# Decoder layer with eight routed experts: routed rows read in squares of 32 and transposed on VectorE

## Reference

```python
x = x + _L0_attn_ref(_layernorm(x), w_qkv, w_out)          # windowed, rotary, 16 heads of 8
x = x + _L0_xattn_ref(_layernorm(x), ctx_1024, Wq, bq, Wk, bk, Wv, bv, Wo, bo, 1)
x = x + _L0_ffn_ref(_layernorm(x), gate_w, w1, w2)

def _L0_ffn_ref(x, gate_w, w1, w2):                        # E = 8 experts, F = 512, TOP_K = 2
    probs = jax.nn.softmax(x @ gate_w, axis=-1)
    topw, topi = jax.lax.top_k(probs, TOP_K)
    topw = topw / topw.sum(axis=-1, keepdims=True)
    combine = (jax.nn.one_hot(topi, E) * topw[..., None]).sum(axis=-2)
    for each expert i:
        h = jax.nn.gelu(x @ w1[i], approximate=False)
        acc = acc + combine[..., i, None] * (h @ w2[i])
    return acc
```

## Time and profile before

| | |
|---|---|
| median of 3 runs | 544.39 us (540.61 to 544.9) |
| profiled execution | 540.55 us, its span 538.7 us |
| mean granted TensorE clock | 0.982 of full speed |
| TensorE busy | 479.2 us, 89% of the span |
| VectorE busy | 380.0 us, 71% |
| ScalarE busy | 338.8 us, 63% |
| GpSimd busy | 306.3 us, 57% |
| DMA queue of SyncE | 35712 packets, 24.69 MB, 16.1% of 16 engines' span |

### The profile page before, as it was taken

One profiled execution on the slowest core, in us unless ns is written; L12 is line 12 of the kernel. 1 busy time (PEld: TensorE's weight loads), 2 busy tenths in 40 slices (PEclk: granted clock), 3 DMA queues, 4 the chain that ended last, 5 costly groups with the idle time before them and its releaser, 6 DMA issues.

```text
span 538.7 us, 30462 instructions
## 1 busy us (share of the span) xinstructions
PE 479.2 (89%) x11885; PEld 397.7 (74%) x11885; DVE 380.0 (71%) x1342; ACT 338.8 (63%) x980; POOL 306.3 (57%) x415
## 2 busy tenths in 40 slices
PE   2589899999999899989899999889987999999992
PEld 2367677777776677767677777666876999999991
DVE  5456688888886734667777777887777666666884
ACT  3357587787786767777888888788532444444440
POOL 2434344544554534357778777776677555555652
PEclk9999999999999988999999999999998999999997
DMA  8312111111111000001111011122122322227264
GB/s 235 89 43 62 41 58 43 56 58 44 54 58 43 29 13 12 15 28 45 33 32 43 30 40 37 34 53 55 49 76 86 93 68 73 74 69 264 56 178 138
DMA packets 40970, 35.09 MB, mean 65 GB/s; under 512 B 6445, under 2 KB 37295, under 8 KB 40896
## 3 DMA queue, kind: packets, MB, share of 16 engines
q1 hardware_dynamic: 35712, 24.69, 16.1%
q0 software_dynamic: 4320, 8.53, 4.7%
q10 hardware_dynamic: 864, 0.86, 0.6%
HBM read 18.63 MB, written 11.68 MB: 56 GB/s over the span
## 4 chain that ended last, share of the span: by engine, by line
PE 79%; issue 7%; DVE 5%; DMA 4%; ACT 2%; POOL 1%; SPq 1%; DVEq 0%; POOLq 0%; ACTq 0%
PE p_scores L1217 11%; PE p_probsT L630 11%; PE p_att_bank L620 8%; PE p_scores L513 7%; PE p_qk L1226 5%; PE p_probsT L1226 5%; PE p_scores L558 5%; PE p_v_bank L583 4%; PE p_scores L506 4%; PE p_att_bank L568 3%; PE p_qk L525 3%; PE p_qk L534 2%; PE p_v_bank L599 2%; PE p_att_bank L935 2%; PE p_qk L526 1%
## 5 line engine op out<-in xcount | busy, mean ns | idle before, releaser
L759 POOL TENSOR_TENSOR k_heads<-qk,consts 128x512 f32<-128x512 f32 x64 | 66.8, 1043 | 95.9 <-DVE qk L821 60.2
L1278 POOL DMA_INDIRECT expert_results<-weighted,result_at x71 | 74.2, 1044 | 53.2 <-DVE weighted L1264 42.7
L657 ACT COPY probsT<-p_probsT 128x512 f32<-128x512 f32 x128 | 75.5, 590 | 23.7 <-PE p_probsT L630 23.4
L860 DVE TENSOR_REDUCE shift<-p_scores 128x8 bf16<-128x512 f32 (+1 forms) x128 | 73.8, 618 | 22.0 <-PE p_scores L513 21.4
L1217 PE MATMUL p_scores<-gotT,w_now 128*128 128x128 f32 x568 | 76.8, 279 | 7.0 <-ACT gotT L1243 4.8
L630 PE MATMUL p_probsT<-consts,probs 128*128 128x128 f32 x512 | 80.7, 281 | 0.4
L663 ACT ACTIVATE probs<-p_scores 128x512 f32<-128x512 f32 x128 | 77.8, 608 | 0.5 <-PE p_scores L558 0.4
L1240 ACT ACTIVATE hidden<-p_scores 128x512 f32<-128x512 f32 x71 | 42.4, 597 | 54.8 <-PE p_scores L1217 54.8
L1217 PEld LDWEIGHTS p_scores<-gotT,w_now 128*128 128x128 f32 x568 | 69.7, 193 | 9.1 <-ACT gotT L1243 6.2
L1003 POOL DMA_INDIRECT sent_rows<-row,slot_u x64 | 64.7, 1011 | 16.6 <-issue 15.2
L716 ACT COPY values<-p_v_bank 32x128 f32<-32x128 f32 x256 | 68.4, 267 | 2.3
(11 more groups left out here) (160 smaller groups left out, 962.8 us busy)
## 6 DMA issues: line engine op xcount, KB each, us to landing
got<-sent_rows SPq DMA_DIRECT2D x71, 66.0 KB, 1.8
swapped<-raw SPq DMA_DIRECT2D x64, 64.0 KB, 1.9
w<-w_in SPq DMA_DIRECT2D x32, 128.0 KB, 2.3
back<-expert_results SPq DMA_DIRECT2D x7, 512.0 KB, 6.0
ctxT<-ctxT_in SPq DMA_DIRECT2D x32, 64.0 KB, 1.9
x<-x_in SPq DMA_DIRECT2D x4, 448.0 KB, 9.4
out<-x SPq DMA_DIRECT2D x7, 256.0 KB, 3.6
expert_results<-weighted,result_at POOLq DMA_INDIRECT x71, 2.4
```

What stands on the lines that cost most here:

```text
L657: nc.scalar.copy(probsT[:, 4 * half:4 * half + 4, :], p_probsT[:, :].rearrange("p (m q) -> p m q", q=P)).then_inc(s_pT, 1)
L759: nc.gpsimd.tensor_tensor(k_heads[:, :, BLK:], qk[:, 1:2, :].to_broadcast([P, G, P]), cv(C_HEAD, G).unsqueeze(2).to_broadcast([P, G, P]), ...
L860: nc.vector.tensor_reduce(shift[:, half * 8:half * 8 + 8], p_scores[:, half * 8:half * 8 + 8, low:WIN], AX.X, ALU.max).then_inc(s_max, 1)
L1278: nc.gpsimd.indirect_dma_start(out=results, out_offset=bass.IndirectOffsetOnAxis(ap=result_at[:, slot:slot + 1], axis=0), in_=weighted[:, ...
```

## The change

The transpose of a block's rows is split between the DMA and VectorE. The tile `got` is now [128, slot, 4, 32]: SyncE reads the 32 columns i of all 128 rows into the partitions 32i to 32i+31, where the partition counts the row within a group of 32, and the free index the group and the column. VectorE's transpose, which works on squares of 32x32, then turns each square in its place and gives `gotT` [feature, row]. The last four columns go to a tile of their own, `got_cols`. So a block has five DMAs, and the semaphore of a slot counts 80 instead of 16. TensorE's transpose, the PSUM tile for it and ScalarE's copy fall away. The multiply by the gate's weight moves from VectorE to ScalarE, and the cast of the result row numbers moves up to block c+2, with a semaphore of its own, `s_at`.

```diff
-        got = sb("got", [P, U, ROW])
+        got = sb("got", [P, U, NBLK, BLK])
+        got_cols = sb("got_cols", [P, U, ROW - P])
...
+        GOT = 16 * (NBLK + 1)
...
             if c >= U:
                 eng.wait_ge(s_y, n + 1 - U)
+                eng.wait_ge(s_at, n + 1 - U)
             first = eng.value_load(table_at(1, n), min_val=0, max_val=E * CAP)
-            eng.dma_start(got[:, slot, :], sent[bass.ds(first, P), :]).then_inc(s_got[slot], 16)
+            for i in range(NBLK):
+                eng.dma_start(got[i * BLK:(i + 1) * BLK, slot, :, :],
+                              sent[bass.ds(first, P), i * BLK:(i + 1) * BLK].rearrange("(j a) b -> a j b", a=BLK)).then_inc(s_got[slot], 16)
+            eng.dma_start(got_cols[:, slot, :], sent[bass.ds(first, P), P:ROW]).then_inc(s_got[slot], 16)
...
         def expert_pe(h, c, _):
...
-            if block_there(h, c, 2):
-                nc.tensor.wait_ge(s_got[(c + 2) % U], 16 * h + 16 * ((c + 2) // U + 1))
-                wait(nc.tensor, s_gT, n + 1)
-                nc.tensor.transpose(p_gotT[c % 2], got[:, (c + 2) % U, 0:P], ident).then_inc(s_gTraw, 1)
...
         def expert_act(h, c, _):
...
-            if block_there(h, c, 2):
-                nc.scalar.wait_ge(s_gTraw, n + 3)
-                nc.scalar.copy(gotT[:, c % 2, :], p_gotT[c % 2]).then_inc(s_gT, 1)
+            if block_there(h, c, -1):
+                slot = (c - 1) % U
+                nc.scalar.wait_ge(s_down, n)
...
+                nc.scalar.wait_ge(s_got[slot], GOT * h + GOT * ((c - 1) // U + 1))
+                nc.scalar.activation(weighted[:, slot, :], p_y[(c - 1) % 2], ACT.Copy, scale=got_cols[:, slot, 0:1]).then_inc(s_y, 1)
...
         def expert_dve(h, c, cols):
...
                 nc.vector.tensor_copy(w1_now[:, c % 2, :], w1[:, bass.ds(at, F)]).then_inc(s_w1_now, 1)
-            if block_there(h, c, -1):
-                slot = (c - 1) % U
-                nc.vector.wait_ge(s_down, n)
...
-                nc.vector.wait_ge(s_got[slot], 16 * h + 16 * ((c - 1) // U + 1))
-                nc.vector.tensor_copy(result_at[:, slot:slot + 1], got[:, slot, P + 1:P + 2])
-                nc.vector.tensor_scalar(weighted[:, slot, :], p_y[(c - 1) % 2], got[:, slot, P:P + 1], None, ALU.mult).then_inc(s_y, 1)
+                slot = (c + 2) % U
+                nc.vector.wait_ge(s_got[slot], GOT * h + GOT * ((c + 2) // U + 1))
+                nc.vector.transpose(gotT[:, c % 2, :], got[:, slot, :, :].rearrange("p j b -> p (j b)")).then_inc(s_gT, 1)
...
+                    nc.vector.wait_ge(s_back[slot], 16 * h + 16 * ((c + 2) // U))
+                nc.vector.tensor_copy(result_at[:, slot:slot + 1], got_cols[:, slot, 1:2]).then_inc(s_at, 1)
...
         def expert_pool(h, c, _):
...
+                nc.gpsimd.wait_ge(s_at, n)
                 nc.gpsimd.wait_ge(s_y, n)
```

More of the change, by code:

```diff
@@ L236, in build @@
         p_hidden = [p_scores[:, i * G:(i + 1) * G, :].rearrange("p g k -> p (g k)") for i in range(2)]
-        p_gotT = [p_scores[:, i * G, :] for i in range(2, 4)]
         p_y = [p_qk[:, 0:P], p_probsT[:, 0:P]]
@@ L273, in build @@
         s_back = [sem(f"results_sent{i}") for i in range(U)]
-        s_gTraw, s_gT, s_up, s_gelu = sem("gotT_in_psum"), sem("gotT_made"), sem("hidden_in_psum"), sem("hidden_made")
+        s_gT, s_at, s_up, s_gelu = sem("gotT_made"), sem("result_at_made"), sem("hidden_in_psum"), sem("hidden_made")
         s_w1_now, s_w2_now, s_down, s_y = sem("w1_copied"), sem("w2_copied"), sem("y_in_psum"), sem("y_weighted")
@@ L1240, in expert_act @@
                 nc.scalar.activation(hidden[:, half, :], p_hidden[half][:, :], ACT.Gelu).then_inc(s_gelu, 1)
-            if block_there(h, c, 2):
-                nc.scalar.wait_ge(s_gTraw, n + 3)
-                nc.scalar.copy(gotT[:, c % 2, :], p_gotT[c % 2]).then_inc(s_gT, 1)
+            if block_there(h, c, -1):
+                slot = (c - 1) % U
+                nc.scalar.wait_ge(s_down, n)
+                if not isinstance(h, int) or c - 1 >= U:
+                    nc.scalar.wait_ge(s_back[slot], 16 * h + 16 * ((c - 1) // U))
+                nc.scalar.wait_ge(s_got[slot], GOT * h + GOT * ((c - 1) // U + 1))
+                nc.scalar.activation(weighted[:, slot, :], p_y[(c - 1) % 2], ACT.Copy, scale=got_cols[:, slot, 0:1]).then_inc(s_y, 1)
         def expert_dve(h, c, cols):
@@ L1255, in expert_dve @@
                 nc.vector.tensor_copy(w1_now[:, c % 2, :], w1[:, bass.ds(at, F)]).then_inc(s_w1_now, 1)
-            if block_there(h, c, -1):
-                slot = (c - 1) % U
-                nc.vector.wait_ge(s_down, n)
-                if not isinstance(h, int) or c - 1 >= U:
-                    nc.vector.wait_ge(s_back[slot], 16 * h + 16 * ((c - 1) // U))
-                nc.vector.wait_ge(s_got[slot], 16 * h + 16 * ((c - 1) // U + 1))
-                nc.vector.tensor_copy(result_at[:, slot:slot + 1], got[:, slot, P + 1:P + 2])
-                nc.vector.tensor_scalar(weighted[:, slot, :], p_y[(c - 1) % 2], got[:, slot, P:P + 1], None, ALU.mult).then_inc(s_y, 1)
+                slot = (c + 2) % U
+                nc.vector.wait_ge(s_got[slot], GOT * h + GOT * ((c + 2) // U + 1))
+                nc.vector.transpose(gotT[:, c % 2, :], got[:, slot, :, :].rearrange("p j b -> p (j b)")).then_inc(s_gT, 1)
+                if not isinstance(h, int) or c + 2 >= U:
+                    nc.vector.wait_ge(s_back[slot], 16 * h + 16 * ((c + 2) // U))
+                nc.vector.tensor_copy(result_at[:, slot:slot + 1], got_cols[:, slot, 1:2]).then_inc(s_at, 1)
             if block_there(h, c, 1):
@@ L1295, in _ @@
             pe.wait_ge(s_probs, 4 * B)
-            for c in (-2, -1, 0):
-                expert_pe(0, c, None)
+            expert_pe(0, 0, None)
             go(steps[B - 1], ALL)
@@ L1331, in _ @@
             steps = {c: kinds[1][1](0, c) for c in range(B - 1, B + 4)}
-            expert_act(0, -2, None)
-            expert_act(0, -1, None)
             nc.scalar.activation(unread[0:1, :], eps[0:1, 0:1], ACT.Gelu)
```

## The result

| | before | after |
|---|---|---|
| median | 544.64 us (540.61 to 546.51, 4 runs) | 630.67 us (630.35 to 631.83, 4 runs) |
| profiled execution, its span | 540.55 us, 538.7 us | 630.95 us, 629.1 us |

The ratio is 1.1655, 95% interval 1.1598 to 1.1713: 86 us slower. The forecast was 620 us, range 602 to 660.

What follows compares the result with a forecast made beforehand. TensorE bounded the expert stage at 1.895 us a block; after, SyncE at 3.21. Last block's DMA 586.6, with pads, read-back and loop 600.2, landing and hand-over 602.5, tail 616.1, clock 617.6; forecast 620 us, range 602 to 660.

Steps and rivals of the forecast that it cites:

- from there SyncE alone sets the pace: Row reads after the first issue at 359.80 us: SyncE's issuing bounds every block, 3.21 us each; chance 0.82.
- 1.097 + 4 x 0.528: SyncE's time per block: 1.097 us for today's single read plus 0.528 for each of four added DMAs, 3.21 us.
- the wait for a second semaphore: SyncE's table load also waits for VectorE's index cast; costed at nothing, since eight slots lie between.
- The loop: The 24 blocks in SyncE's loop have register operations of their own, about 0.1 us each, 2.4 us together.
- The end: Tail from the last block's first projection to the span's end: 13.6 us, expected to stay as before.
- swing between its two levels: TensorE in the expert stage, idle 1.4 us of each 3.2, alternates between low and full clock and keeps up.
- the 19 us for the low level throughout: TensorE at low clock for the 53 blocks after the pads: 0.36 us each, 19 us, used for the range.
- the clock's term: 1.5 us added to the sum for TensorE running the last block at the low clock level.
- the hand-over of the last block: After the last read lands, transpose and hand-over to TensorE take 0.5 us.
- The packets: Rival: 720 small packets a block make the DMA engines the bound, from 71 ns a packet; chance 0.09.
- The hidden issue: Rival: SyncE's added issues stay hidden, each under 0.17 us, and only TensorE's gain shows: 534.5 us; chance 0.04.
- the faster rival: SyncE's issues stay hidden behind TensorE's work, leaving its gain of 6.0 us, so 534.5 us; chance 0.04.

## Why the prediction was right, and where its sum was off

**The bound.** The step "from there SyncE alone sets the pace" held from the first read to the last, and it was tested from both sides: five issues alone cost 1.16 to 1.18, the rest alone gives 0.987.

**The pace of SyncE.** The sum had 3.21 us a block from 1.097 + 4 x 0.528, and measured are 3.16 undisturbed: the stripes issue in 317 ns, not 333, while the wait for a second semaphore was indeed free. The loop adds 0.16, not 0.1. The last issue nevertheless came at 611.0, not 600.2. The term that was missing: between 358.94 and 609.02 us lie 70 blocks; without the pads (8.8) and the read-back (2.8) that is 238.5 us, or 3.41 each, while 46 at 3.16 and 24 at 3.32 are 225. The other 13.4 us are stretches: 8.0 of them are issues that lasted longer than their medians, as from 366.31 on (up to 1.79 us for one), the rest is time between issues. The row of before had shown a maximum of 873 ns; the median was taken for all.

**The end.** Timeline of the last block after the change:

```profile
612.62 0.31 DVE L1265 STREAM_TRANSPOSE gotT<-got 128x128 f32<-128x128 f32 x1 [1.92 <-DMA got_cols<-sent_rows]
...
612.98 0.97 PEld L1223 LDWEIGHTS p_scores<-gotT,w_now 128*128 128x128 f32 x8 [1.34 <-DVE gotT L1265]
...
617.55 0.97 POOL L1284 DMA_INDIRECT expert_results<-weighted,result_at  x1 [0.30 <-issue]
...
622.13 0.80 SPq L446 DMA_DIRECT2D back<-expert_results  x2
```

From the last first projection to the end it is 16.1 us, where 13.6 were carried over from the earlier trace rows. The chain differs in one place: from the start of the last result's scatter to the read-back that waits for it are 4.6 us (617.55 to 622.13), before 2.3 (529.66 to 531.93). Two read-backs of 512 KB are issued 3.5 us ahead of it now; before, they had gone 10 us ahead. That they delayed it is a reading, not tested.

**The clock.** The forecast that TensorE would swing between its two levels and keep up held. These are first projections behind the pads, behind the read-back, and of the last block:

```profile
435.01 2.08 PE L1223 MATMUL p_scores<-gotT,w_now 128*128 128x128 f32 x8 [10.11 <-DVE gotT L1265]
...
573.51 2.08 PE L1223 MATMUL p_scores<-gotT,w_now 128*128 128x128 f32 x8 [7.13 <-DVE gotT L1265]
...
612.98 1.16 PE L1223 MATMUL p_scores<-gotT,w_now 128*128 128x128 f32 x8 [1.15 <-DVE gotT L1265]
```

After waits of 10.11 and 7.13 us the eight records together last 2.08 us, where those of the last block last 1.16. The granted clock is 0.50 from 430 to 435 us, and the windows of 15 us around the two waits show 0.77 and 0.89, means of the two levels (1.2 and 2.4 GHz). From 495 to 555 us, where TensorE was busy for about 9 of 15 us and no wait was over 1.7 us, the clock stayed at 1.00. The low stretches cost nothing here, because SyncE set the pace and its wait for slots stayed at 0.3 us. The 1.5 us for a last block at the low level were not there, and the 19 us for the low level throughout went into the range without need.

**The sum as a whole.** The span was forecast at 617.6 us and came out at 629.1. The first issue came 0.9 earlier, the pace took off 3.5 us, the clock's term 1.5 and the hand-over of the last block 0.3; the stretches added 13.4, the end 2.5, the loop 1.4 and the read-back issues 0.4. So the missing term is larger than the whole miss, and others hid part of it.

**VectorE.** The transpose, assumed at 0.30 us, takes 0.309:

```profile
L1265 DVE STREAM_TRANSPOSE gotT<-got 128x128 f32<-128x128 f32 x71 | 21.9, 309 | 108.0 <-DMA got_cols<-sent_rows 107.9
```

Its 108.0 us of idle time ahead of it are SyncE's time seen from VectorE; taken as a cost of the transpose it would point to the wrong engine.

**The rivals.** The packets: the queue's row after is

```profile
q1 hardware_dynamic: 76608, 24.71, 17.0%
```

17.0% x 16 x 629.1 / 76608 = 22 ns a packet, far from the 71 at which they would have decided; 45 on each engine are 1.0 us of 3.3. The Trainium skill's remark on transfers under 512 B (DMA: Bandwidth & Descriptors, "Specifications") thus was no bound here, with some 2 us of difference between 528 B and 128 B pieces. The hidden issue: the Trainium skill's sentence on the same page that starting a DMA is usually small beside the DMA ("Issuing engines are not separate DMA queues") is true of one (0.33 us beside 1.8 to landing) and misled for five in a row. What the faster rival got right is its price: 6 us forecast for TensorE, and 6.8 measured (5.4 to 8.5) as soon as the issue is single again.

## What to carry to other kernels

When a transfer is cut into several to save an engine work, count the instructions of the engine that issues them first: here one DMA more costs 0.5 us of SyncE, and the room was 1.895 - 1.10 = 0.8 us a block, of which two issues use nearly all. A queue that is idle in the profile because it waits for free buffers has that much room and no more; once its work exceeds the consumer's, it stops waiting for buffers (0.3 us here), and more of them have nothing to shorten. And a gain can be real and still be lost: the transpose's share of TensorE was worth some 6 us, but its replacement needed four more issues, where the stage could hide hardly one more.

## What the runs showed that was not expected

The length of an issue depends on the shape in an odd way: 316 to 317 ns for 16 to 96 partitions, 333 for 128, but 477 in the median for 64 partitions (468 at least). That fits the swap of odd and even partitions, also 64 in number, at 464 at least, so its stride alone need not be the reason. The 128 pieces of 16 B took 352 ns after the change and 333 in the kernel with five DMAs by columns. Why 64 differs, and what made these 352, stays open.

SyncE's issues stretch at times without waiting for anything that the profile shows: of the 14 issues of block reads that took over 400 ns, 10 lie before 405 us, while the attention's transfers and GpSimd's scatters still ran, and there the first eight reads took 3.75 us a block (358.94 to 388.94) instead of 3.16. What stretches them was not tested.

The read-back reaches further than its own issues. While it runs, the DMA share is 1.01 after the change (565 to 570 us) and 1.02 before (490 to 495). Behind it TensorE waited 7.13 us for rows after the change, and only 0.57 before, when SyncE had room to read ahead.
